# A four-stage transformer block on one core: the multiplication in the row quantisation moved from VectorE to GpSimd

## The chip, the cores and the metric

The kernel runs on one core of a Trainium2 chip (trn2). The metric is the device time of one execution in microseconds (us), the median over the runs. Engines: TensorE (PE in the profile, with its weight loads as PEld), VectorE (DVE), ScalarE (ACT), GpSimd (POOL) and SyncE (SP), which issues the DMAs here. Each has its own instruction stream, and they meet through semaphores.

## The reference

Eight batches of 512 rows x 512 columns pass through four layers, each with a layer norm ahead of it and a residual sum behind it:

```python
x = x + L0_xattn(layernorm(x), ctx, mask)      # 16 heads of 32, 77 keys
x = x + L0_ffn(layernorm(x), packed ternary w) # rows quantised to 8 bits
x = x + L1_xattn(layernorm(x), ctx)            # 16 heads of 64, 77 keys
x = x + L1_ffn(layernorm(x), w_freq)           # product with a matrix in frequency space
```

The second layer is the one that the change touches. For each row:

```python
act_scale = 127.0 / max(max(abs(x)), 1e-5)
x_dq = clip(round(x * act_scale), -128.0, 127.0) / act_scale
y = x_dq @ w.T + bias                          # w is ternary times one scale
```

## The kernel before

A batch has four tiles of 128 rows (t = 0 to 3). All other layers split their operands into a high and a low float16 part and multiply three times (`products`, lines 167 to 172); the ternary layer multiplies small whole numbers in bfloat16, once.

**Order of the work.** The program is a hand-written schedule. A batch's round has 18 slots (`NS`), and each engine walks through the same list `SLOTS` in its own program. Slots 0 to 7 have a unit of the first attention (stage X), slots 10 to 17 one of the second attention (stage Y, of the batch before), slots 8 and 9 none. A unit is a tile's scores for half of the heads: scores on TensorE, maxima on VectorE, exponentials on ScalarE, sums on VectorE, normalisation on GpSimd (`normalise`, line 644), a high part on ScalarE (line 783), a low part on VectorE (line 1180) or, for units in `LOW_BY_POOL`, on GpSimd (line 649), then a transposing DMA. `FILLS` puts matrix products into the slots, and their results are drained one slot later, by ScalarE and VectorE or by VectorE alone (the residual sum, line 1112, with the row statistics, line 1052 and `ln_group`, lines 1058 to 1068).

**Layer norms.** VectorE makes the variance, GpSimd the reciprocal root and the shift (`rstd_of`, lines 635 and 637). The tables `APPLY`, `LOWER` and `BIAS` say in which slot a pair of tiles is normalised, lowered and given its bias. An entry is (j, pair): j is the layer (0 to 3), the pair 0 means tiles 0 and 1, the pair 2 means tiles 2 and 3. For j = 1, the quantised layer, `APPLY` and `LOWER` have (1, 0) in slot 8 and (1, 2) in slot 13. `BIAS` has (1, 0) in slot 9 and (1, 2) together with (2, 2) in slot 13, four additions of 128x512 on GpSimd (line 666).

**The quantisation.** ScalarE writes the normalised rows of a pair into `xn` (line 800; 128 x 2 x 512 float32; one buffer for all layers). VectorE's `quantise` (lines 1070 to 1085) finds the largest magnitude of each row (line 1077), bounds it (1078), makes the scale for the result (1079), the reciprocal (1080) and the step (1081), multiplies each tile by its step and adds the rounding constant (1083, two instructions), and takes the constant off again, with the bound at 127, while it writes bfloat16 into `xh` (1085). `step` is a fence: the instruction raises a semaphore and VectorE waits for it. The last one raises `ln_lowered`, for which SyncE's transposing DMA into `qiT` waits (line 522), and behind that TensorE's product (line 1337).

**GpSimd's slot.** It does, in this order: normalise the unit of the slot before; `rstd_of`; the rows that it normalises itself (`rows`, line 657, a tensor-scalar of 128x512 with a column for each operand, into the same `xn`); the low part of the unit two slots back; the biases. In slot 8 the `rstd_of` is that of the next batch's first layer norm, for whose variance VectorE works just ahead of `quantise`.

Of the kernel before, what the change touches and what calls it, by code (L numbers as in the profile page):

```python
# [9 lines left out]
ALU = mybir.AluOpType  # L10
# [137 lines left out]
def listed(table, g):  # L148

    i, s = SLOTS[g]  # L150
    out = [(j, pair, i - ln_lag(j, pair)) for j, pair in table.get(s, [])]
    return [e for e in out if there(e[2])]
# [7 lines left out]
GROUPS = {(j, b, t): n for n, (j, t0, w, b) in enumerate(sum((groups_at(g) for g in range(len(SLOTS))), [])) for t in range(t0, t0 + w)}  # L160
APPLIED = {e: n for n, e in enumerate(sum((listed(APPLY, g) for g in range(len(SLOTS))), []))}
POOL_ROWS = {e: n for n, e in enumerate([e for e in APPLIED if e[:2] in ROWS_BY_POOL])}
FIRST_ROWS = [e for e in APPLIED if e[0] == 0 and e[2] == 0]
BIASED = {e: n for n, e in enumerate(sum((listed(BIAS, g) for g in range(len(SLOTS))), []))}

# [81 lines left out]
def layers(nc, k, x, scr_k0, scr_k1, scr_v0, scr_v1, out, inputs):  # L247

    here = ExitStack()
    with here:  # L250
# [3 lines left out]
        def sem(name):  # L254
            return here.enter_context(nc.semaphore(name))
# [39 lines left out]
        ln_var, rstd_ready, ln_ready, ln_applied, ln_lowered, biased = (sem(n) for n in (  # L295
            "ln_var", "rstd_ready", "ln_ready", "ln_applied", "ln_lowered", "biased"))
        rows_ready = sem("rows_ready")
        rows_turned = [sem(f"rows_turned{i}") for i in range(2)]
        absmax_ready, allmax_ready, scale_ready, hi_done, lo_done = (sem(n) for n in (
            "absmax_ready", "allmax_ready", "scale_ready", "hi_done", "lo_done"))  # L300
# [122 lines left out]
        def unit_at(g):  # L423

            return SLOT_UNIT[g] if 0 <= g < len(SLOTS) else None
# [181 lines left out]
        def _(pool):  # L607
# [44 lines left out]
            def rows(j, pair, b):  # L652
# [4 lines left out]
                    ins = pool.tensor_scalar(xn[:, t - pair, :], xs(b)[:, t, :], rstd[:, j, t:t + 1], shift[:, j, t:t + 1], ALU.mult, ALU.add)  # L657
                ins.then_inc(rows_ready, 1)

            def add_bias(j, pair, b):  # L660
                pool.wait_ge(ln_lowered if (j, pair) in ROWS_BY_DVE else ln_applied, APPLIED[j, pair, b] + 1)
                if (j, pair) in ROWS_BY_POOL:
                    pool.wait_ge(rows_ready, POOL_ROWS[j, pair, b] + 1)
                bias = {1: "bf0", 2: "bo", 3: "bf1"}[j]
                for t in (pair, pair + 1):
                    ins = pool.tensor_tensor(xs(b)[:, t, :], xs(b)[:, t, :], k[bias][:, :], ALU.add)  # L666
                ins.then_inc(biased, 1)
# [17 lines left out]
            for g, (i, s) in enumerate(SLOTS):  # L685
                if unit_at(g - 1):
                    normalise(*unit_at(g - 1))
                if (i, s) == (0, 0):
                    all_reduce("WQ1")
                if (i, s) == (1, 4):  # L690
                    all_reduce("WO")
                for e in groups_at(g):
                    if e[0] != 0 or e[3] != 0:
                        rstd_of(*e)
                for e in later(APPLY, g):
                    if e[:2] in ROWS_BY_POOL:
                        pool.wait_ge(ln_ready, GROUPS[e[0], e[2], e[1]] + 1)
                        rows(*e)
                if unit_at(g - 2) and unit_at(g - 2)[:2] in LOW_BY_POOL:
                    probs_low(*unit_at(g - 2))  # L700
                for e in listed(BIAS, g):
                    add_bias(*e)

# [153 lines left out]
        def _(dve):  # L857
# [212 lines left out]
            def quantise(t, b):  # L1070
# [7 lines left out]
                step(dve.tensor_scalar(amax[:, pair], amax[:, pair], 1e-5, None, ALU.max))  # L1078
                dve.tensor_scalar(cscale[:, pair], amax[:, pair], f[:, F_WSC:F_WSC + 1], None, ALU.mult)
                step(dve.reciprocal(ascale[:, pair], amax[:, pair]))  # L1080
                step(dve.tensor_scalar(ascale[:, pair], ascale[:, pair], 127.0, None, ALU.mult))
                for j in (t, t + 1):
                    ins = dve.tensor_scalar(xn[:, j - t, :], xn[:, j - t, :], ascale[:, j:j + 1], MAGIC, ALU.mult, ALU.add)  # L1083
                step(ins)
                dve.tensor_scalar(quantised(n), xn[:, :, :], MAGIC, 127.0, ALU.subtract, ALU.min).then_inc(ln_lowered, 1)

            def rows_low(j, pair, b):
# [433 lines left out]
```

## Time and profile before

| | |
|---|---|
| median of 3 runs | 1170.33 us (1170.12 to 1173.37) |
| the profiled execution's time | 1169.09 us |
| its span in the trace | 1167.3 us |
| mean granted TensorE clock | 0.91 |
| PE busy | 957.4 us (82%) |
| DVE busy | 898.2 us (77%) |
| ACT busy | 634.9 us (54%) |
| POOL busy | 492.7 us (42%) |

The rows are all of the one profiled execution; its time is 1.2 us under the median, and its span leaves out 1.8 us around it. A batch's round takes some 110 us in the middle of the run: the early calls of `quantise` for batches 4 and 5 start at 635.25 and 743.51 us. Busy shares are averages over stages with different limits, so the chain of waits and the rows in order of time tell more. In a row of the timeline the bracket at the end is the idle time of the engine before it and what ended that.

### The profile page before, as it was taken

Reading aid. Unit: us, or ns where it says so; the run is one execution under the profiler, and the core shown is the slowest. Engines: PE = TensorE matmul, PEld = TensorE weight load, DVE = VectorE, ACT = ScalarE, POOL = GpSimd, SP = SyncE. Lnnn points to the kernel's source line nnn. Section 1 sums busy time; section 2 is a strip of 40 time slices with the busy share of each in tenths; the row PEclk is TensorE's granted clock in tenths of the full one; section 3 lists DMA queues with packets and bytes.
Section 4 is the critical chain, followed back from the end, with each engine's and each line's share of the span. In section 5 each row is a group of like instructions: output and inputs, shape, how many; then the busy total and the mean of one; then the engine's idle time right before and its main releaser. Section 6 shows DMA issues by size and latency. Waiting matters only on the chain.

```text
span 1167.3 us, 17877 instructions
## 1 busy us (share of the span) xinstructions
PE 957.4 (82%) x6211; PEld 508.7 (44%) x6227; DVE 898.2 (77%) x1704; ACT 634.9 (54%) x1748; POOL 492.7 (42%) x437
## 2 busy tenths in 40 slices
PE   1896994693777997898799889979997898599694
PEld 0443463352343554454454445544554455344341
DVE  8777379537989799979987998899789978835732
ACT  2333174233577658657763776477558656614701
POOL 0224024111646267337723762475267336802603
PEclk9988997895699998999899989989998999699797
DMA  9623025543846747585648656746856483551612
GB/s 368 195 86 108 1 67 137 121 116 74 144 88 105 134 84 128 96 167 110 116 102 146 100 107 122 147 89 120 141 110 123 90 143 69 111 103 25 118 39 72
DMA packets 379026, 131.95 MB, mean 113 GB/s; under 512 B 365148, under 2 KB 370812, under 8 KB 375609
## 3 DMA queue, kind: packets, MB, share of 16 engines
q1 hardware_dynamic: 378937, 130.82, 54.7%
q8 instruction: 49, 0.80, 0.3%
q14 instruction: 40, 0.33, 0.1%
HBM read 35.14 MB, written 15.96 MB: 44 GB/s over the span
## 4 chain that ended last, share of the span: by engine, by line
DVE 35%; PE 24%; DMA 10%; ACT 9%; POOL 8%; SPq 8%; issue 7%; ACTq 0%; POOLq 0%; DVEq 0%
PE wb L170 6%; PE wb L171 6%; PE wb L172 6%; DMA prT<-ph 6%; DVE ph L1180 4%; ACT pr L770 3%; DVE mx L1158 3%; SPq L494 3%; PE wb L1307 2%; DVE xr L1112 2%; DVE stats L1052 2%; POOL xr L666 2%; DVE xn L1083 2%; DVE parts L862 2%; ACT xn L800 2%
## 5 line engine op out<-in xcount | busy, mean ns | idle before, releaser
L644 POOL TENSOR_TENSOR pr<-pr,sm 128x616 f32<-128x616 f32 x128 | 166.1, 1298 | 289.9 <-DVE sm L1175 283.0
L770 ACT ACTIVATE pr<-scores,mx,factor 128x77 f32<-128x77 f32 x576 | 229.6, 425 | 21.6 <-DVE mx L1161 18.4
L170 PE MATMUL wb<-xT,wq_hl 128*128 128x512 f16 x384 | 150.8, 393 | 9.6 <-DVE qc L1105 4.2
L171 PE MATMUL wb<-xT,wq_hl 128*128 128x512 f16 x384 | 150.6, 392 | 0.0
L172 PE MATMUL wb<-xT,wq_hl 128*128 128x512 f16 x384 | 149.6, 390 | 0.0
L783 ACT ACTIVATE ph<-pr 128x618 f16<-128x618 f32 x128 | 93.5, 732 | 97.0 <-DMA prT<-ph 75.6
L635 POOL TENSOR_TENSOR rstd<-var,mhalf 128x2 f32<-128x2 f32 (+1 forms) x48 | 51.2, 1067 | 221.4 <-DVE var L1068 221.4
L770 ACT ACTIVATION_READ_ACCUMULATOR pr<-scores,mx,factor 128x1 f32 x576 | 123.9, 215 | 0.0
L1112 DVE SCALAR_TENSOR_TENSOR xr<-wb,factor,xr 128x512 f32<-128x512 f32 x72 | 53.3, 740 | 71.7 <-PE wb L172 71.7
L1158 DVE TENSOR_REDUCE mx<-scores 128x8 f32<-128x616 f32 x128 | 101.1, 790 | 5.7 <-PE scores L172 5.6
L170 PE MATMUL scores<-k1b,qc 128*128 128x154 f16 x256 | 61.0, 256 | 49.3 <-DVE qc L1105 29.1
L170 PE MATMUL wb<-wo_hl,qc 128*128 128x512 f16 x256 | 97.1, 379 | 0.0
L172 PE MATMUL wb<-wo_hl,qc 128*128 128x512 f16 x256 | 97.1, 379 | 0.0
L171 PE MATMUL wb<-wo_hl,qc 128*128 128x512 f16 x256 | 97.1, 379 | 0.0
L730 ACT ACTIVATE qc<-wb,bq_s 128x512 f16<-128x512 f32 x64 | 43.7, 686 | 81.6 <-PE wb L172 81.6
L774 ACT ACTIVATE pr<-pr,factor 128x616 f32<-128x616 f32 x56 | 45.4, 811 | 76.5 <-DVE pr L1166 76.4
L1096 DVE TENSOR_TENSOR xh<-xn,xh 128x1024 f16<-128x1024 f32 x48 | 69.4, 1446 | 20.4 <-ACT xh L797 9.9
L1180 DVE SCALAR_TENSOR_TENSOR ph<-pr,ph 128x618 f16<-128x618 f32 x80 | 83.4, 1043 | 1.0 <-ACT ph L783 0.7
L1307 PE MATMUL wb<-prT,v1b 103*64 103x512 f16 x576 | 72.1, 404 | 10.3 <-DMA prT<-ph 8.0
L797 ACT ACTIVATE xh<-xr,shift,rstd 128x512 f16<-128x512 f32 x72 | 56.1, 804 | 39.0 <-POOL shift L637 26.7
L666 POOL TENSOR_TENSOR xr<-xr,bf_b 128x512 f32<-128x512 f32 x48 | 72.9, 1539 | 8.2 <-ACT xh L797 7.1
L1337 PE MATMUL wb<-tern,qiT 128*128 128x512 bf16 x112 | 38.8, 475 | 38.5 <-DMA qiT<-xh 21.2
(218 smaller groups left out, 2502.6 us busy)
## 6 DMA issues: line engine op xcount, KB each, us to landing
xr<-in_x SPq DMA_DIRECT2D x6, 1024.0 KB, 6.1
out_x<-xr SPq DMA_DIRECT2D x6, 1024.0 KB, 5.2
prT<-in_dft SPq DMA_DIRECT2D x1, 3072.0 KB, 22.2
k1b<-scr_k SPq DMA_DIRECT2D x16, 154.0 KB, 6.8
scr_v<-k1b SPq DMA_DIRECT2D x9, 256.0 KB, 3.2
scr_k<-k1b SPq DMA_DIRECT2D x7, 308.0 KB, 3.1
xr<-in_wf SPq DMA_DIRECT2D x2, 1024.0 KB, 10.6
x<-in_x SPq DMA_DIRECT2D x2, 1024.0 KB, 10.7
```

The lines of the kernel that those rows point to most:

```text
L170: pe.matmul(out, lhs(0), rhs(0), start=start, stop=False, **kw)
L171: pe.matmul(out, lhs(0), rhs(1), start=False, stop=False, **kw)
L172: return pe.matmul(out, lhs(1), rhs(0), start=False, stop=stop, **kw)
L644: pool.tensor_tensor(v, v, s, ALU.mult).then_inc(probs_ready, 1)
L666: ins = pool.tensor_tensor(xs(b)[:, t, :], xs(b)[:, t, :], k[bias][:, :], ALU.add)
L770: ins = act.activation(pr[U % 3][:, h // 4, cols], sc[:, U % 2, h // 4, cols], ACT.Exp, bias=mx[:, U % 4, h:h + 1], scale=k["factor"][:, f ...
L783: act.activation(ph[:, U % 2, 0, :, :, 0:CH], pr[U % 3][:, :, 0:GKP].rearrange("p g (c n) -> p g c n", c=3), ACT.Copy, scale=1.0 if (stage ...
L1096: dve.tensor_tensor(xh[:, n % 2, :, 1, :], xn[:, :, :], xh[:, n % 2, :, 0, :], ALU.subtract).then_inc(ln_lowered, 1)
L1112: dve.scalar_tensor_tensor(out=xs(b)[:, t, :], in0=wb[:, n % WB, :], scalar=factor, in1=xs(b)[:, t, :], op0=ALU.mult, op1=ALU.add).then_in ...
L1158: step(dve.tensor_reduce(m, s, AX.X, ALU.max))
L1180: dve.scalar_tensor_tensor(out=ph[:, U % 2, 1, :, :, 0:CH], in0=pr[U % 3][:, :, 0:GKP].rearrange("p g (c n) -> p g c n", c=3), scalar=PS, ...
L1307: return pe.matmul(bank[column:column + H1, :], v1b[0:CH, h, g, slot, :], prT[0:CH, :, g // 2, h1, g % 2, c, :], start=start, stop=stop, s ...
```

## The change

GpSimd gets a function `round_rows` that does the two multiplications of a pair in place in `xn`. VectorE raises `step_known` with the step and then waits for `rows_rounded`. In GpSimd's slot the new call stands behind the low part and ahead of the biases. The table `QUANTISED` only counts the calls.

```diff
+QUANTISED = {e[1:]: n for n, e in enumerate([e for e in sum((listed(LOWER, g) for g in range(len(SLOTS))), []) if e[0] == 1])}
...
+        step_known, rows_rounded = sem("step_known"), sem("rows_rounded")
...
+            def round_rows(t, b):
+                pool.wait_ge(step_known, QUANTISED[t, b] + 1)
+                for j in (t, t + 1):
+                    ins = pool.tensor_scalar(xn[:, j - t, :], xn[:, j - t, :], ascale[:, j:j + 1], MAGIC, ALU.mult, ALU.add)
+                ins.then_inc(rows_rounded, 1)
...
                 if unit_at(g - 2) and unit_at(g - 2)[:2] in LOW_BY_POOL:
                     probs_low(*unit_at(g - 2))
+                for j, pair, b in later(LOWER, g):
+                    if j == 1:
+                        round_rows(pair, b)
                 for e in listed(BIAS, g):
                     add_bias(*e)
...
                 step(dve.reciprocal(ascale[:, pair], amax[:, pair]))
-                step(dve.tensor_scalar(ascale[:, pair], ascale[:, pair], 127.0, None, ALU.mult))
-                for j in (t, t + 1):
-                    ins = dve.tensor_scalar(xn[:, j - t, :], xn[:, j - t, :], ascale[:, j:j + 1], MAGIC, ALU.mult, ALU.add)
-                step(ins)
+                dve.tensor_scalar(ascale[:, pair], ascale[:, pair], 127.0, None, ALU.mult).then_inc(step_known, 1)
+                dve.wait_ge(rows_rounded, QUANTISED[t, b] + 1)
                 dve.tensor_scalar(quantised(n), xn[:, :, :], MAGIC, 127.0, ALU.subtract, ALU.min).then_inc(ln_lowered, 1)
```

GpSimd's order in slot 13 (the pair (1, 2) of a batch in the middle of the run) was, from the low part of a unit on through the biases of layers 1 and 2 to the next slot's normalisation:

```order
L649 TENSOR_TENSOR ph<-pr,ph 128x6x103 [waits probs_hi]
L666 TENSOR_TENSOR xr<-xr,bf_b 128x512 [waits ln_applied]
L666 TENSOR_TENSOR xr<-xr,bf_b 128x512
L666 TENSOR_TENSOR xr<-xr,bo_b 128x512 [waits ln_applied]
L666 TENSOR_TENSOR xr<-xr,bo_b 128x512
L644 TENSOR_TENSOR pr<-pr,sm 128x2x308 [waits sums_ready]
```

and is now, with every line number of GpSimd's program 2 to 8 higher:

```order
L651 TENSOR_TENSOR ph<-pr,ph 128x6x103 [waits probs_hi]
L665 TENSOR_SCALAR xn<-xn,ascale 128x512 [waits step_known]
L665 TENSOR_SCALAR xn<-xn,ascale 128x512
L674 TENSOR_TENSOR xr<-xr,bf_b 128x512 [waits ln_applied]
L674 TENSOR_TENSOR xr<-xr,bf_b 128x512
L674 TENSOR_TENSOR xr<-xr,bo_b 128x512 [waits ln_applied]
L674 TENSOR_TENSOR xr<-xr,bo_b 128x512
L646 TENSOR_TENSOR pr<-pr,sm 128x2x308 [waits sums_ready]
```

The four additions and all behind them now stand behind the wait for the step. VectorE's end of `quantise` in slot 13 and the next unit's first operations were:

```order
L1079 TENSOR_SCALAR cscale<-amax,factor 128x2 [waits dve_step]
L1080 RECIPROCAL ascale<-amax 128x2
L1081 TENSOR_SCALAR ascale<-ascale 128x2 [waits dve_step]
L1083 TENSOR_SCALAR xn<-xn,ascale 128x512 [waits dve_step]
L1083 TENSOR_SCALAR xn<-xn,ascale 128x512
L1085 TENSOR_SCALAR xh<-xn 128x1024 [waits dve_step]
L1158 TENSOR_REDUCE mx<-scores 128x8 [waits scores_full]
```

and are now:

```order
L1090 TENSOR_SCALAR cscale<-amax,factor 128x2 [waits dve_step]
L1091 RECIPROCAL ascale<-amax 128x2
L1092 TENSOR_SCALAR ascale<-ascale 128x2 [waits dve_step]
L1094 TENSOR_SCALAR xh<-xn 128x1024 [waits rows_rounded]
L1167 TENSOR_REDUCE mx<-scores 128x8 [waits scores_full]
```

Two instructions left VectorE, and its last one of the call waits for GpSimd.

## Rows read from the trace of the kernel before

**Rows 1.** The page's part 4: the chain that ended last, shares by engine
```profile
DVE 35%; PE 24%; DMA 10%; ACT 9%; POOL 8%; SPq 8%; issue 7%; ACTq 0%; POOLq 0%; DVEq 0%
```
**Rows 2.** The chain in order of time, whole run (start us, us, what)
```profile
633.72 1.51 ACT xn L800 x2
```
**Rows 3.** The same chain, 606 to 680 us (batch 4, both calls)
```profile
637.25 0.90 DVE xn L1083 x2
...
641.14 0.07 issue
...
668.45 1.85 DVE xn L1083 x2
...
671.05 3.08 DMA qiT<-xh
```
**Rows 4.** Timeline, VectorE and GpSimd, early call, batch 4 (start us, us, engine...)
```profile
635.25 1.22 DVE L1077 TENSOR_REDUCE amax<-xn 128x2 f32<-128x1024 f32 x1 [2.37 <-ACT xn L800]
...
638.16 0.69 DVE L1085 TENSOR_SCALAR xh<-xn 128x1024 bf16<-128x1024 f32 x1
...
641.21 1.01 POOL L635 TENSOR_TENSOR rstd<-var,mhalf 128x4 f32<-128x4 f32 x1 [5.69 <-DVE var L1068]
```
**Rows 5.** Timeline, VectorE and GpSimd, late call and after, batch 4
```profile
664.36 1.20 DVE L1077 TENSOR_REDUCE amax<-xn 128x2 f32<-128x1024 f32 x1
...
667.29 1.12 DVE L1081 TENSOR_SCALAR ascale<-ascale 128x2 f32<-128x2 f32 x1
...
670.33 0.69 DVE L1085 TENSOR_SCALAR xh<-xn 128x1024 bf16<-128x1024 f32 x1
...
672.48 0.16 DVE L1174 TENSOR_SCALAR sm<-sm 128x8 f32<-128x8 f32 x1
...
674.61 0.17 DVE L1065 TENSOR_SCALAR mean<-mean 128x2 f32<-128x2 f32 x1
...
664.67 2.49 POOL L666 TENSOR_TENSOR x<-x,bf_b 128x512 f32<-128x512 f32 x2
667.12 2.49 POOL L666 TENSOR_TENSOR xr<-xr,bo_b 128x512 f32<-128x512 f32 x2
672.96 1.22 POOL L644 TENSOR_TENSOR pr<-pr,sm 128x616 f32<-128x616 f32 x1 [3.35 <-DVE sm L1175]
```
**Rows 6.** Instructions on tile xn (ns min/median/max, first and last start)
```profile
L657 POOL TENSOR_SCALAR xn<-xr,rstd,shift x36: 758/767/1417, 201.1 to 1142.2; 128x512 f32<-128x512 f32 x36
```
**Rows 7.** Timeline, early call of batch 1, and a VectorE row released by GpSimd
```profile
314.58 1.69 DVE L1085 TENSOR_SCALAR xh<-xn 128x1024 bf16<-128x1024 f32 x1
...
314.16 1.56 POOL L649 TENSOR_TENSOR ph<-pr,ph 128x618 f16<-128x618 f32 x1 [0.82 <-ACT ph L783]
...
1006.82 0.80 DVE L1166 TENSOR_TENSOR pr<-scores,mx 128x616 f32<-128x616 f32 x1 [0.57 <-POOL ph L649]
...
1004.42 2.30 POOL L649 TENSOR_TENSOR ph<-pr,ph 128x618 f16<-128x618 f32 x1
```
**Rows 8.** Timeline, both calls of batch 0
```profile
194.70 2.59 POOL L649 TENSOR_TENSOR ph<-pr,ph 128x618 f16<-128x618 f32 x2
...
200.22 0.69 DVE L1085 TENSOR_SCALAR xh<-xn 128x1024 bf16<-128x1024 f32 x1
...
221.26 2.48 POOL L666 TENSOR_TENSOR x<-x,bf_b 128x512 f32<-128x512 f32 x2 [6.35 <-ACT xn L800]
...
222.73 1.05 DVE L1078 TENSOR_SCALAR amax<-amax 128x2 f32<-128x2 f32 x1
...
225.26 0.69 DVE L1085 TENSOR_SCALAR xh<-xn 128x1024 bf16<-128x1024 f32 x1
```
**Rows 9.** TensorE's waits; windows (busy of PE, PEld, DVE, ACT, POOL; clock; DMA; GB/s)
```profile
639.58 0.39 PE L170 MATMUL wb<-xT,wq_hl 128*128 128x512 f16 x1 [1.25 <-DVE xr L1112]
...
674.26 1.86 PE L1337 MATMUL wb<-tern,qiT 128*128 128x512 bf16 x4 [3.18 <-DMA qiT<-xh]
...
639.50:642.00 2.50, 2.42 (x12) 1.13 (x13) 2.36 (x11) 0.00 (x0) 0.79 (x1) 1.00 0.64 120
674.20:680.00 5.80, 5.74 (x22) 3.00 (x23) 5.59 (x16) 5.79 (x17) 4.73 (x6) 0.50 0.31 65
```

## The prediction

> **What bounds the kernel now.** I read the chain of waits first, because no engine is busy all the time. It passes from engine to engine and spends its largest share on VectorE [rows 1]. So a microsecond of VectorE counts where the chain is on VectorE, and one of GpSimd only where VectorE or the chain waits for it. I then read the chain in order of time over one batch, to see where the quantisation lies on it. Each batch calls `quantise` twice: for rows 0 and 1 in slot 8 (the **early call**) and for rows 2 and 3 in slot 13 (the **late call**). The chain enters the early call from ScalarE's normalised rows in batches 2 to 6, five times (one of them in [rows 2]), runs through its multiplication [rows 3] and on by the residual sum and the row statistics to GpSimd. It also runs through the late call [rows 3]; in batches 4 and 5 it leaves by the transposing DMA to TensorE, in batches 1, 2, 3, 6 and 7 it stays on VectorE. Last I set the VectorE and GpSimd rows of both calls side by side (batch 4 stands for all). In the early call GpSimd is idle and VectorE's operations go at their own length [rows 4]. In the late call GpSimd adds biases for 5 us and VectorE's tensor-scalars are stretched: from the start of the reduction to the start of the last operation it is 5.97 us, against 2.91 us in the early call [rows 4, 5]. The 3.06 us between them are waiting inside VectorE's rows. The reader should see how: a tensor-scalar of VectorE that starts while a GpSimd operation runs ends only about when that one does (the 1.12 us row on two numbers per partition), and it never happens while GpSimd is idle.
>
> **The change, part by part.**
> *Removed from VectorE*: per call two 128x512 multiplications and the fence behind them, 0.90 us [rows 3] when alone.
> *Added to GpSimd*: per call two operations of the same shape. The nearest row is GpSimd's own tensor-scalar of 128x512 float32, 0.767 us each [rows 6]; with one constant instead of a second column I take the same, so 1.53 us.
> *Added waits*: VectorE to GpSimd costs 0.07 us [rows 3]; back, 0.10 us: the VectorE row that waited for GpSimd starts at 1006.82, the GpSimd operation ended at 1004.42 + 2.30 = 1006.72 [rows 7]. Behind VectorE's wait stands its whole program; behind GpSimd's, in the late call, stand four bias additions.
>
> *Early call, batches 2 to 6.* GpSimd is idle there, its next work waits for VectorE anyway. VectorE's path from the end of the step to the last operation was 0.90 us and becomes 0.07 + 1.53 + 0.10 = 1.70 us; less some 0.05 us for the fences that go with it, **+0.75 us** each, on the chain: +3.75 us. Bounds: +0.2 us if GpSimd did it at VectorE's own 0.45 us a piece [rows 3], +1.7 us if it took as long as its two-input additions, 1.25 us (half of a pair in [rows 5]). I take the row of its own form, which lies between them.
>
> *Early call, batch 1.* GpSimd's next operation there, the low part of another unit, ran at 314.16 and the last operation of the call beside it, 1.69 us instead of 0.69 [rows 7]. The step is known at about 313.65 (0.93 us, two multiplications and a fence, ahead of that operation); the rounding then lasts to 315.25; the low part (1.30 us, half of [rows 8]'s pair) starts at once, VectorE 0.10 us later and so behind it: end about 317.2 against 314.58 + 1.69 = 316.27, +0.9 us.
>
> *Early call, batch 0.* Two low parts and two bias additions of GpSimd lie on it, and the call ends at 200.22 + 0.69 = 200.9 [rows 8]. Now GpSimd waits after the first low part, which ends at 196.0 (half of the pair); the step follows two small operations later, 196.3, rounding to 197.9, second low part to 199.2, last operation to 199.9: -1.05 us. Batch 0, late call: there are only two additions, from 221.26, and they stretch one small operation to 1.05 us; the call ends at 225.26 + 0.69 = 225.95 [rows 8]. Now the step is known 0.9 us earlier, at 223.45, the rounding ends at 225.05, and the last operation waits for the first addition behind it, 225.05 + 1.25 + 0.69 = 227.0: +1.0 us. These two cancel. In batch 7 the chain is on TensorE at the early call: 0.
>
> *Late call, the others.* GpSimd now stands still until the step is known, so the reduction and the small operations run at their own length: the step is ready 1.96 us after the start, at 666.3 instead of 668.4. The rounding ends at 667.9. Then the four bias additions that had run from 664.67 [rows 5] start, without a pause, as GpSimd's operations do back to back in those rows; VectorE needs 0.10 us to notice, and its last operation waits for the first addition: end at 667.9 + 1.25 + 0.69 = 669.8, against 670.33 + 0.69 = 671.02. **The stretch of 3.06 us becomes a gain of 1.2 us at this point**, for the rounding costs 1.7 instead of 1.85 with its stretch, and the last operation takes the wait over. What is late next: the other additions now run from 669.1, held up 0.7 us by VectorE's last operation (the 1.56 us row of [rows 7] shows such a hold-up), to about 673.5, instead of being over at 669.6. VectorE's next small tensor-scalar, at 672.48 before [rows 5], comes at 671.3 into the third addition and ends at 672.4, 0.25 us ahead; the one in the row statistics, at 674.61 before, comes at 674.35 under the normalisation of probabilities, which started at 672.96 and now starts at 673.5 and ends at 674.7. The lead is then 0 to 0.1 us. So on VectorE the gain is given back within one slot: -0.1 us in each of batches 1, 2, 3, 6 and 7, -0.5 us. By the transposing DMA the 1.2 us arrive at TensorE, which waited 3.18 us for it in batch 4 [rows 9]; but VectorE, 0.1 us ahead, is close behind TensorE there, so I take half, -0.5 us in each of batches 4 and 5, -1.0 us. Bounds for these seven: 0 and -8 us (the whole 1.2 us each).
>
> GpSimd's normalisation ends 0.5 us later and ScalarE with it; I found no wait behind it that this would lengthen. DMAs are neither added nor moved in any queue. Order on the other three engines is untouched.
>
> *Sum*: the terms in their order are +3.75 + 0.9 - 1.05 + 1.0 - 0.5 - 1.0 = **+3.1 us**. The profiled execution took 1169.09 us, so 1172.2 there; it lies 1.24 us under the median of the runs, which gives 1173.4 us against 1170.33.
>
> The Trainium skill, "GPSIMD Engine Reference", section 4.1 Engine selection, sends elementwise work to VectorE, but calls one-input operations on GpSimd "roughly line-rate". At 512 elements per partition that would be some 0.53 us for one operation (an estimate from that page's words and VectorE's 0.96 GHz), and the sum would be nearer +1 us, inside the forecast's own range. The row of this kernel says 0.767 us, and the sum goes by the row.
>
> **Rivals.**
> *A, VectorE gets in first (faster).* Decides: whether the last operation of the late call starts before GpSimd's first bias addition. Then it ends at 668.7 and not 669.8, and with the same working the lead after the row statistics is about 1.1 us: seven late calls -7.7 us; batch 0 early -2.2 and late 0, batch 1 early -0.3, the five early calls +3.75: -6.4 us, 1163.9. Against it: the additions need no semaphore that is open by then, and follow back to back in [rows 5], while VectorE has to be woken over 0.10 us. The Trainium skill, "SBUF — State Buffer", section Who interferes with whom, says that the two engines share a port pair as an exclusive lock, and that whoever issues first holds it for its whole instruction; the 1.69 us of [rows 7] agree with it. Chance 0.14.
> *B, TensorE loses its clock at the early call (slower, well beyond the forecast).* TensorE waits 1.25 us for VectorE's residual sum there [rows 9], which becomes 2.0 us; it kept the full clock (1.00, 2.4 GHz) behind 1.25 us but ran at the level of 1.2 GHz (0.50) for 5.8 us behind 3.18 us [rows 9]. 5.8 us at half clock are 2.9 us lost; five times on the chain, with the +3.1, gives up to 1188. From which wait on the clock falls no row between 1.25 and 3.18 us says; 2.0 is nearer the harmless one. Chance 0.12.
> *C, the waits are hidden.* The chain was beside other paths with as much length, and the 0.75 us vanish in slack, as would the lead of the late calls: 1170.3. For it: in batch 7 it is TensorE's. Against it: five of eight batches have it on the chain. Chance 0.12.
> *D, TensorE gains at the late call.* Its wait of 3.18 us shrinks to 2.0 us and in batches 4 and 5 the 5.8 us at half clock [rows 9] go away: -2.9 us twice, 1167.6. Chance 0.12.
>
> **How the numbers follow.** Forecast 0.50, between 1170 and 1177 by its bounds. A measurement of this kernel can tell about 0.3%, 3.5 us: faster is below 1166.8, slower above 1173.8. The forecast lies just inside "same": 0.28 same, 0.22 slower. A gives 0.12 faster and 0.02 same, B 0.12 slower, C 0.10 same and 0.02 faster, D 0.06 each of faster and same. Together faster 0.20, same 0.46, slower 0.34. The range goes from the better part of A to the lower half of B: 1164.5 to 1180.
>
> **What would show it.** After the change: the early call's last operation starts about 3.7 us after the reduction's start (2.91 now); the late call's ends about 5.5 us after it (6.66 now) and shows 1.7 to 1.9 us instead of 0.69 as its own length; the small tensor-scalar that follows shows about 1.1 us instead of 0.16; GpSimd's rounding rows show 0.77 us. A last operation of 0.69 us in the late call means rival A. A granted clock of 0.5 right behind the early call means B, and none behind the late one D. If the GpSimd row is far from 0.77 us, the sum is off from its first term.

## The result, and the profile after

| | before | change |
|---|---|---|
| median, measured side by side | 1172.53 us (16 runs, 1169.38 to 1177.05) | 1176.31 us (16 runs, 1173.82 to 1179.00) |
| ratio to before | | 1.0034, 95% interval 1.0021 to 1.0046 |
| the profiled execution | 1169.09 us, span 1167.3, clock 0.910 | 1176.54 us, span 1174.2, clock 0.907 |

The change makes the kernel slower by 0.34%, 3.8 us, just over what a measurement of it can tell from nothing. The forecast was a sum of +3.1 us, called just inside "same". The size is close; the reason turned out to be another one. The two profiled executions lie 6.9 us apart, more than the medians: a profile shows where time goes, and the medians say how much. Of the executions timed below, one of the kernel e3_bias14 took 2022.66 us and is left out of its row.

The page of the kernel after, its parts 1 and 4 (engines; shares of the chain by engine, against [rows 1]):

```profile
PE 960.9 (82%) x6211; PEld 508.8 (43%) x6227; DVE 880.6 (75%) x1672; ACT 636.1 (54%) x1748; POOL 522.1 (44%) x469
...
DVE 33%; PE 25%; POOL 11%; ACT 8%; DMA 8%; issue 7%; SPq 7%; POOLq 0%; ACTq 0%; DVEq 0%
```

VectorE lost 17.6 us of busy time, GpSimd gained 29.4 us, and the chain moved the same way: VectorE 35% to 33%, GpSimd 8% to 11%. So VectorE has less to do and the kernel is slower; the share of an engine answers nothing here.

The new instructions of GpSimd, from the view of one source line of the kernel after:

```profile
L665 POOL TENSOR_SCALAR xn<-xn,ascale x32: 690/691/696, 196.6 to 1000.0; 128x512 f32<-128x512 f32 x32
its engine sat idle before it (us, times) until:
  DVE ascale L1092: 28.5, 16
who waited for it (us, times):
  DVE xh L1094: 24.0, 16
```

One takes 0.691 us, to within 6 ns in all 32, not the 0.767 us of GpSimd's normalisation [rows 6]. VectorE waited 24.0 us for it in 16 calls, 1.5 us each.

The early call of batch 4, timeline of VectorE and GpSimd of the kernel after (against [rows 4]):

```profile
639.12 1.22 DVE L1088 TENSOR_REDUCE amax<-xn 128x2 f32<-128x1024 f32 x1 [2.45 <-ACT xn L811]
...
640.91 0.17 DVE L1092 TENSOR_SCALAR ascale<-ascale 128x2 f32<-128x2 f32 x1
642.58 0.69 DVE L1094 TENSOR_SCALAR xh<-xn 128x1024 bf16<-128x1024 f32 x1 [1.50 <-POOL xn L665]
...
641.18 1.36 POOL L665 TENSOR_SCALAR xn<-xn,ascale 128x512 f32<-128x512 f32 x2 [1.87 <-DVE ascale L1092]
```

From the reduction to the last operation it is 3.46 us, against 2.91 us: +0.55 us. The step ends at 641.08, GpSimd starts 0.10 us later, and VectorE starts 0.04 us after GpSimd's 642.54.

Batch 4 does not stand for all early calls. In batch 3 GpSimd is at a low part when the kernel after calls `quantise`, and stretches a small operation from 0.17 to 1.00 us:

```profile
528.66 1.00 DVE L1089 TENSOR_SCALAR amax<-amax 128x2 f32<-128x2 f32 x1
...
528.33 1.32 POOL L651 TENSOR_TENSOR ph<-pr,ph 128x618 f16<-128x618 f32 x1
```

Before, that happened in the early calls of batches 2 and 5, after, in those of batches 2, 3 and 5. From the end of the step on it is +0.55 us in all of them, but batch 3's call as a whole got 1.35 us longer.

The late call of batch 4 and what follows, the same view (against [rows 5]):

```profile
668.82 1.20 DVE L1088 TENSOR_REDUCE amax<-xn 128x2 f32<-128x1024 f32 x1
...
670.59 0.17 DVE L1092 TENSOR_SCALAR ascale<-ascale 128x2 f32<-128x2 f32 x1
672.25 1.75 DVE L1094 TENSOR_SCALAR xh<-xn 128x1024 bf16<-128x1024 f32 x1 [1.50 <-POOL xn L665]
...
675.46 0.92 DVE L1183 TENSOR_SCALAR sm<-sm 128x8 f32<-128x8 f32 x1
...
678.01 0.77 DVE L1073 TENSOR_TENSOR mean<-stats 128x2 f32<-128x2 f32 x1
...
678.95 0.17 DVE L1076 TENSOR_SCALAR mean<-mean 128x2 f32<-128x2 f32 x1
...
670.86 1.36 POOL L665 TENSOR_SCALAR xn<-xn,ascale 128x512 f32<-128x512 f32 x2 [1.69 <-DVE ascale L1092]
672.18 2.94 POOL L674 TENSOR_TENSOR x<-x,bf_b 128x512 f32<-128x512 f32 x2
675.08 2.50 POOL L674 TENSOR_TENSOR xr<-xr,bo_b 128x512 f32<-128x512 f32 x2
677.54 1.22 POOL L646 TENSOR_TENSOR pr<-pr,sm 128x616 f32<-128x616 f32 x1
```

The reader should see four things. The step, which had stretched to 1.12 us, is at its own 0.17 us. The last operation has the stretch now, 1.75 us instead of 0.69, since GpSimd's first addition starts at 672.18 and VectorE's operation at 672.25. The call ends at 674.00, 5.18 us after its start, against 6.66 us. And the lead of 1.48 us is gone behind it: two small operations took 0.92 us beside the third addition and 0.77 us beside the normalisation behind them, and the first tensor-scalar of the row statistics stands 10.13 us after the call's start, against 674.61 - 664.36 = 10.25 us before. In both calls of this batch the local picture is the predicted one.

What had not been looked at is TensorE behind the late call. Some 30 us behind the late call's start TensorE has done the 36 products of the second attention's probabilities with its values (slot 17) and waits until VectorE has drained one of their output banks; then it starts the ternary product of the fourth tile. Its row of batch 4, and a window of 4 us from 30.0 us behind the call's start. Columns of a window: length, busy PE, PEld, DVE, ACT, POOL, granted clock, DMA share, GB/s. The kernel before:

```profile
694.32 0.81 PE L1337 MATMUL wb<-tern,qiT 128*128 128x512 bf16 x3 [1.76 <-DVE qc L1103]
...
694.36:698.36 4.00, 4.00 (x22) 2.11 (x22) 3.86 (x13) 3.99 (x18) 0.61 (x2) 1.00 0.72 137
```

The kernel after, and the stretch that answers to [rows 9]'s half clock:

```profile
698.46 1.06 PE L1346 MATMUL wb<-tern,qiT 128*128 128x512 bf16 x2 [3.72 <-DVE qc L1112]
...
678.82:684.82 6.00, 5.87 (x35) 2.79 (x32) 5.83 (x14) 6.00 (x18) 5.21 (x6) 1.00 0.32 62
...
698.82:702.82 4.00, 4.00 (x14) 1.93 (x13) 3.60 (x12) 2.46 (x11) 0.33 (x1) 0.50 0.36 68
```

After [rows 9]'s wait of 3.18 us for the transposing DMA TensorE ran at the 1.2 GHz level. In the kernel after, that wait is no longer there and the clock is 1.00 in that stretch. But TensorE, earlier now (its 36 products end 25.9 us behind the call's start, not 28.2), waits 3.72 us instead of 1.76 us at the next place, for a bank that VectorE frees only 0.3 us earlier, and behind it the clock is at 0.50: 14 matmuls in 4 us where there had been 22. Round 4 (from batch 4's late call to batch 5's) takes 111.6 us after and 109.1 us before.

The half clock about the late call did not go away in batch 4, though, it moved forward. These windows go from 4 us ahead of the call's start to 16 us behind it, before and after:

```profile
660.36:680.36 20.00, 13.04 (x64) 7.10 (x65) 18.52 (x36) 15.24 (x50) 13.70 (x13) 0.74 0.70 120
...
664.82:684.82 20.00, 16.12 (x80) 8.56 (x80) 17.07 (x34) 15.25 (x49) 15.61 (x15) 0.74 0.70 121
```

The mean clock is 0.74 in both, and TensorE does 80 matmuls in place of 64. Nor is batch 4 the typical one. Mean granted clock in that window, in the one from 26 to 40 us behind the call's start, and the round:

| batch | about the call: before, after | 26 to 40 us: before, after | round: before, after |
|---|---|---|---|
| 2 | 0.74, 0.74 | 1.00, 0.76 | 108.3, 110.7 us |
| 3 | 0.74, 0.83 | 0.76, 0.88 | 111.8, 110.9 us |
| 4 | 0.74, 0.74 | 1.00, 0.76 | 109.1, 111.6 us |
| 5 | 0.74, 0.91 | 1.00, 0.88 | 110.1, 111.1 us |
| 6 | 0.74, 0.74 | 0.88, 1.00 | 106.4, 105.7 us |

Both kernels have as much half clock in these windows, some 62 us in the five batches. What differs is the place: about the late call or behind the wait at 30 us. Before, the second place has it in batches 3 and 6, after, in batches 2 to 5. The wait of 1.76 us was one of batches 4 and 5 only; in batches 2, 3 and 6 it was 3.53 to 3.71 us already before the change.

The starts of the last late call are 989.92 us before and 997.26 us after; from there to the end of the span it is 177.4 and 176.9 us. So the difference of the two profiles arises in the rounds: +1.3, +2.2, +2.4, -0.9, +2.6, +0.9 and -0.6 us for those of batches 0 to 6.

### The profile page after: what moved, and what is told of

Its sections match the earlier page's. It is cut to its first block, busy times and chain, and to the rows that moved or that the text cites. A ratio compares the mean times of both kernels' runs of the same rounds, so it can differ in the third digit from the quotient of the medians.

```text
span 1174.2 us, 17877 instructions
## 1 busy us (share of the span) xinstructions
PE 960.9 (82%) x6211; PEld 508.8 (43%) x6227; DVE 880.6 (75%) x1672; ACT 636.1 (54%) x1748; POOL 522.1 (44%) x469
## 4 chain that ended last, share of the span: by engine, by line
DVE 33%; PE 25%; POOL 11%; ACT 8%; DMA 8%; issue 7%; SPq 7%; POOLq 0%; ACTq 0%; DVEq 0%
PE wb L171 7%; PE wb L172 6%; PE wb L173 6%; DVE ph L1189 3%; ACT pr L781 3%; DVE mx L1167 3%; DVE stats L1063 3%; SPq L496 3%; PE wb L1316 3%; DMA prT<-ph 3%; POOL xr L674 2%; DVE xh L1105 2%; DVE parts L873 2%; DVE xr L1121 2%; POOL xn L665 2%
## 5 line engine op out<-in xcount | busy, mean ns | idle before, releaser
L1105 DVE TENSOR_TENSOR xh<-xn,xh 128x1024 f16<-128x1024 f32 x48 | 72.7, 1515 | 21.5 <-ACT xh L808 9.9
L674 POOL TENSOR_TENSOR xr<-xr,bf_b 128x512 f32<-128x512 f32 x48 | 75.5, 1594 | 8.0 <-ACT xh L808 7.1
L1063 DVE BATCH_NORM_STATS2 stats<-xr 128x6 f32<-128x512 f32 x96 | 64.7, 690 | 4.4 <-DMA xr<-in_x 1.8
```

The lines of the kernel that those rows point to most:

```text
L1063: last = dve.bn_stats(stats[:, j, t, :], xs(b)[:, t, :])
L1105: dve.tensor_tensor(xh[:, n % 2, :, 1, :], xn[:, :, :], xh[:, n % 2, :, 0, :], ALU.subtract).then_inc(ln_lowered, 1)
```

## The experiments

Theories, all made after the result, and the third only after the first four runs. **Theory 1**: the handover in the early calls is the loss. **Theory 2**: the loss is in the late call, where GpSimd stands still until the step is known, so that its additions and what follows come later. Beside it stands the prediction's rival A: the stretched last operation keeps the gain away. **Theory 3**: each local gain or loss only moves TensorE against VectorE, and what it costs is the clock behind TensorE's wait 30 us behind the late call. Rounds, waits and dips are read from one profiled execution of each kernel. "Dip" below is a stretch of a granted clock of about 0.5 there. Every kernel was timed beside the kernel before, whose medians there were 1172.83 us (e1 to e9) and 1173.48 us (e10 to e12). They ran in three groups on different chips, so across groups the ratios are what to compare.

| run | what | median (runs) | ratio to before, 95% interval |
|---|---|---|---|
| the change | | 1176.31 (16) | 1.0034, 1.0021 to 1.0046 |
| e1_early | only the early call moved | 1177.81 (6) | 1.0044, 1.0027 to 1.0060 |
| e2_late | only the late call moved | 1176.41 (12) | 1.0033, 1.0018 to 1.0049 |
| e3_bias14 | before, biases one slot later | 1170.55 (11) | 0.9984, 0.9972 to 0.9997 |
| e4_dve_first | change, VectorE let in first | 1171.67 (12) | 0.9982, 0.9968 to 0.9995 |
| e6_after_bias14 | change, biases one slot later | 1178.60 (8) | 1.0045, 1.0030 to 1.0060 |
| e7_after_busy | change, some products twice | 1170.51 (12) | 0.9983, 0.9968 to 0.9998 |
| e8_before_busy | before, the same products twice | 1172.56 (12) | 0.9991, 0.9978 to 1.0003 |
| e9_bias6_14 | before, biases in slots 6 and 14 | 1169.26 (8) | 0.9969, 0.9953 to 0.9984 |
| e10_bias6_14_busy | e9 with the products twice | 1165.31 (6) | 0.9940, 0.9918 to 0.9962 |
| e11_dve_first_busy | e4 with the products twice | 1166.49 (10) | 0.9953, 0.9938 to 0.9968 |
| e12_early_busy | e1 with the products twice | 1171.68 (12) | 0.9995, 0.9981 to 1.0008 |

### The two halves of the change: e1_early and e2_late

`quantise` takes the new way only where t is 0 (e1) or 2 (e2), and GpSimd rounds only then:

```diff
+                if t == 0:
+                    dve.tensor_scalar(ascale[:, pair], ascale[:, pair], 127.0, None, ALU.mult).then_inc(step_known, 1)
+                    dve.wait_ge(rows_rounded, b + 1)
+                else:
+                    step(dve.tensor_scalar(ascale[:, pair], ascale[:, pair], 127.0, None, ALU.mult))
+                    for j in (t, t + 1):
+                        ins = dve.tensor_scalar(xn[:, j - t, :], xn[:, j - t, :], ascale[:, j:j + 1], MAGIC, ALU.mult, ALU.add)
+                    step(ins)
```

Expected of e1_early:

> Only the early call's multiplication (rows 0 and 1, slot 8) goes to GpSimd, the late call is as before. Theory 1 (the loss is the early call's handover of 0.55 to 0.75 us on the chain, the late call gives its gain back): the last operation of the early call starts 0.55 us later after the reduction, the late call is unchanged at 6.66 us, and the time is 3 to 4 us above before (ratio about 1.003), as large as the whole change's. Theory 2 (the loss is GpSimd's standing still in the late call, which delays its additions and the normalisation behind them): within 1 us of before.

Expected of e2_late:

> Only the late call's multiplication (rows 2 and 3, slot 13) goes to GpSimd. Theory 1: the call ends 1.47 us earlier after its start (5.19 instead of 6.66 us), the row statistics behind it only 0.1 us earlier, and the time is within 1.5 us of before (ratio 0.999 to 1.001). Theory 2: 3 to 4 us above before (1.003).

Measured: 1177.81 and 1176.41 us. The first is what theory 1 expected, and 1 us more, the second what theory 2 did, so neither can be the whole. Each half alone costs as much as both together. They do not add, which a sum of handovers and stretches would have to. Inside the calls each half does what it did in the change: e1's early call takes 0.55 us more and its late call 6.66 us as before, e2's late call 5.19 us. So the place of the loss is not in the calls. Both halves have what the change has, a wait 30 us behind the late call (2.74 to 3.71 us) with, mostly, a dip behind it; batch 4 of e2_late, timeline and window:

```profile
698.91 1.06 PE L1352 MATMUL wb<-tern,qiT 128*128 128x512 bf16 x2 [3.71 <-DVE qc L1118]
...
699.28:703.28 4.00, 4.00 (x14) 1.97 (x13) 3.59 (x12) 2.45 (x11) 0.34 (x1) 0.50 0.38 72
```

In e1_early there is a dip in all of batches 2 to 6, in e2_late in batches 2, 4, 5 and 6. Their longest rounds, 113.8 and 112.8 us, are round 5 of each, and there the clock falls a second time: behind the early call of batch 6, after waits of TensorE of 2.61 and 2.11 us. That is the prediction's rival B, which the change itself shows nowhere in batches 2 to 6.

The rounds can be sorted by it. In the kernels before and after, e1, e2 and e4 (below), rounds 2 to 5 with a dip take 111.1 us on average (16 rounds), those without one 109.1 us (4 rounds). A dip goes with some 2 us.

### Taking GpSimd out of the late call: e3_bias14, and on the change: e6_after_bias14

The same line in both:

```diff
-BIAS = {9: [(1, 0)], 10: [(3, 0)], 13: [(1, 2), (2, 2)], 15: [(3, 2)], 16: [(2, 0)]}
+BIAS = {9: [(1, 0)], 10: [(3, 0)], 14: [(1, 2), (2, 2)], 15: [(3, 2)], 16: [(2, 0)]}
```

Expected of e3_bias14:

> The kernel before, with the biases of slot 13 (four additions on GpSimd) moved to slot 14; no multiplication moves. If the 3.06 us by which the late call is longer than the early one are VectorE waiting for GpSimd's additions, the late call takes 3.6 to 3.9 us instead of 6.66 in every batch, with all its rows at their own length. What the time does depends on where the additions land: GpSimd's next normalisation is up to 5 us later. If that is hidden, 5 to 15 us below before; if it is on the chain, 5 us or more above.

Expected of e6_after_bias14:

> The whole change with the additions of slot 13 moved to slot 14, so that nothing of GpSimd stands behind the rounding of the late call. The last operation shows 0.69 us and the late call takes 4.15 us, as the early one. Against the kernel before with the additions in slot 14 it has both handovers of 0.55 us and nothing in return: 4 to 9 us above that kernel (some 1175 to 1180).

e3_bias14, late call of batch 4 (timeline, VectorE):

```profile
664.03 1.20 DVE L1077 TENSOR_REDUCE amax<-xn 128x2 f32<-128x1024 f32 x1
665.26 0.17 DVE L1078 TENSOR_SCALAR amax<-amax 128x2 f32<-128x2 f32 x1
665.47 0.23 DVE L1079 TENSOR_SCALAR cscale<-amax,factor 128x2 f32<-128x2 f32 x1
665.60 0.16 DVE L1080 RECIPROCAL ascale<-amax 128x2 f32<-128x2 f32 x1
665.80 0.17 DVE L1081 TENSOR_SCALAR ascale<-ascale 128x2 f32<-128x2 f32 x1
666.92 0.69 DVE L1085 TENSOR_SCALAR xh<-xn 128x1024 bf16<-128x1024 f32 x1
```

The call takes 3.58 us instead of 6.66, every row at its own length: the 3.06 us in VectorE's rows of [rows 5] were waiting for GpSimd's additions. The row statistics end 7.67 us after the call's start instead of 10.74. That is some 3 us earlier per batch in seven batches, and 0.9 us in batch 0, and the kernel gains 2 us in all (0.9984), which is neither of the outcomes expected. On the change the same edit loses instead of gains: 1.0045, with the late call at 4.12 us. In that profile the last late call starts 4.0 us earlier than in the change (993.28 against 997.26), and the stretch behind it is 4.4 us longer (181.3 us against 176.9). In e3_bias14 it is long too, 180.5 us. Why the end of the run grows when batch 7's biases come a slot later I did not find; it stays open.

e9_bias6_14 moves the two pairs to different slots, 6 and 14:

```diff
-BIAS = {9: [(1, 0)], 10: [(3, 0)], 13: [(1, 2), (2, 2)], 15: [(3, 2)], 16: [(2, 0)]}
+BIAS = {6: [(2, 2)], 9: [(1, 0)], 10: [(3, 0)], 14: [(1, 2)], 15: [(3, 2)], 16: [(2, 0)]}
```

> The kernel before with the additions of slot 13 taken apart: the attention's bias (2,2) goes to slot 6 of the same round, where GpSimd waits, the quantised layer's bias (1,2) to slot 14. The late call takes 3.6 us in place of 6.66 as with both moved to slot 14, and GpSimd's next normalisation is 2.5 instead of 5 us later. 3 to 8 us below before.

Measured 0.9969, the end 174.8 us long and the late call at 3.58 us. But its rounds 2 to 5 take 109.3, 110.8, 109.2 and 110.1 us, not less than before's 108.3, 111.8, 109.1 and 110.1: there is a wait of 3.3 us and a dip in all of them.

### Letting VectorE in first: e4_dve_first (rival A)

GpSimd waits, behind its rounding, for that rounding to be written, before it goes on to the additions:

```diff
                 ins.then_inc(rows_rounded, 1)
+                pool.wait_ge(rows_rounded, QUANTISED[t, b] + 1)
```

> The whole change, and GpSimd waits for its own rounding semaphore before it goes on, so that VectorE's last operation starts before GpSimd's first addition (rival A of the prediction made true). If it does, the last operation of the late call shows 0.69 us instead of 1.75, the late call ends at about 4.2 us instead of 5.19 after its start, and the row statistics 1 us earlier than with the change. By the prediction's rival A that is worth about 7 to 9 us against the change as made (some 4 us below before); if the lead is lost again behind the call, within 2 us of the change.

Late call of batch 4, timeline of VectorE and GpSimd:

```profile
663.40 1.20 DVE L1089 TENSOR_REDUCE amax<-xn 128x2 f32<-128x1024 f32 x1
...
666.84 0.69 DVE L1095 TENSOR_SCALAR xh<-xn 128x1024 bf16<-128x1024 f32 x1 [1.49 <-POOL xn L665]
...
673.88 0.16 DVE L1080 TENSOR_TENSOR var<-var,half 128x2 f32<-128x2 f32 x1
...
666.89 2.99 POOL L675 TENSOR_TENSOR x<-x,bf_b 128x512 f32<-128x512 f32 x2
```

Now VectorE starts 0.05 us ahead of the addition and takes 0.69 us, and GpSimd's pair shows the hold-up, 2.99 us instead of 2.49 [rows 5]. The call ends 4.13 us after its start. Yet the variance is ready 10.64 us after it, where the change has 10.63: the additions behind take this lead too. So rival A's mechanism works and its price of 1.1 us per late call doesn't arrive. The kernel is nevertheless 4.6 us faster than the change by the medians, some 6 us by the ratios. In the profiles 3.6 us of it lie between the late calls of batches 0 and 1 (117.4 us against 121.0), where the early call, too, ends 1.1 us earlier (5.24 against 6.35 us). So the stretched last operations cost something, but in batches 0 and 1 and not round by round. How 1.1 us there become 3.6 us no run shows.

### Holding the clock: e7_after_busy and e8_before_busy

The last 18 of the 36 products of probabilities with values that TensorE does just ahead of the long wait are done twice (`pair` in this edit counts output banks, not tiles), in the change (e7) and in the kernel before (e8). The first results are overwritten by the second; TensorE has about 2 us more to do per batch.

```diff
+                if pair == 2:
+                    for n, (h, h1) in enumerate(((0, 0), (0, 1), (1, 0))):
+                        head(o, 0, 0, h, h1, 0, n == 0, n == 2)
+                        head(o, H1, 1, h, h1, 0, n == 0, n == 2)
...
```

Expected of e7_after_busy:

> The whole change, and TensorE does the 18 products of the third and fourth output bank of the second attention twice (the second time from scratch, so the result is the same). It makes TensorE busy for 2 us more in the stretch in which it waits 3.5 to 3.7 us per round for VectorE's drain, some 26 to 29.5 us behind the start of the late call. Theory 3 (the change loses by TensorE's clock there: the late call's transpose now arrives early, TensorE no longer waits at +10 us, runs ahead, and waits once and longer at +29.5 us, behind which its clock is at 0.5 for 4 to 6 us on the chain): the wait is 1.5 to 2 us, the granted clock behind it is 1.00 in all rounds, and the time is 5 to 9 us below the change's in spite of the added work. Theory 1 (only the handover counts): no gain, 0 to 5 us above the change.

Expected of e8_before_busy:

> The kernel before with the same added products. Theory 3: in the profile of before the clock falls behind this wait in two or three rounds of five, so the gain is half as large, 2 to 5 us below before. Theory 1: 0 to 5 us above before.

e7_after_busy, batch 4, the same row and window as above:

```profile
693.24 1.04 PE L1356 MATMUL wb<-tern,qiT 128*128 128x512 bf16 x4 [1.37 <-DVE qc L1112]
...
694.00:698.00 4.00, 4.00 (x24) 2.15 (x22) 3.86 (x13) 2.89 (x13) 0.69 (x1) 1.00 0.36 68
```

The wait is 1.37 us, the clock 1.00, 24 matmuls in 4 us instead of 14. The wait is 1.36 or 1.37 us without a dip in all of batches 2 to 6, in both kernels. With more work for TensorE the change is 5.8 us faster, at 0.9983. Its rounds 2 to 5 take 109.2, 109.3, 109.0 and 109.5 us, where the change had 110.7, 110.9, 111.6 and 111.1: 7.2 us less together, of which 3.6 us are given back behind the last late call (180.5 us against 176.9), perhaps because batch 7's doubled products find no such wait to lie in.

The kernel before with the same products is at 0.9991, no more than 1 us below before, where theory 3 had expected 2 to 5 us. Its rounds 2 to 5 are 108.7, 108.9, 108.8 and 109.2 us, 3.7 us less together than before's, most of it in round 3, the one with a dip; behind the last late call it is 4.5 us longer (181.8 us against 177.3), so that little is left. With the clock held at this place in both, the change is not slower than the kernel before: 0.9983 against 0.9991, and the intervals overlap. Its rounds are 0.3 to 0.5 us longer, near the early call's 0.55 us. TensorE's busy time points the same way: the same 144 added matmuls raise it by 12.5 us in the kernel before (957.4 to 969.9) and by 5.0 us in the change (960.9 to 965.9).

This pair speaks for theory 3: with the wait filled, the 3.8 us are gone. Two limits remain. The products shorten the wait and remove the dip at once, so no run holds the clock and leaves the wait as it is. And the mean granted clock of a whole execution doesn't show the loss: it is 0.912 in the 16 executions of the change and 0.912 in the 77 of the kernel before beside e1 to e12, and it rises to 0.921 in e7 and 0.918 in e8. As in the table by batch, the clock of batches 2 to 6 is at 0.50 for as long before as after, and it is the place that would have to make the difference; e8 is at 0.50 for as long as before about every late call, and its rounds are short.

### With the clock held: e12_early_busy, e11_dve_first_busy, e10_bias6_14_busy

The edits are those of e1, e4 and e9, each with the products twice.

Expected of e12_early_busy:

> Only the early call's rounding by GpSimd, and the 18 output products of pair 2 done twice. If the clock made the early call's part of the change dear (1177.8 us without the added products), then here the clock is 1.00 in all rounds and what is left is the handover, 0.5 us in each of five or six batches, +3 us on the 1172.6 of the kernel before with the same products less what batches 0 and 1 gain: 1172 to 1176 us. If the handover itself costs more than its own length, over 1177 us with the clock at 1.00.

Measured 0.9995 where the early half without the products was at 1.0044. Rounds 2 to 5: 109.1, 109.5, 109.2, 109.3 us. It stands with e8_before_busy's 0.9991; the early call's handovers, 0.55 us each, are not to be told from nothing in the whole, though its rounds are 0.1 to 0.6 us longer than e8's. Theory 1 falls as the main cause.

Expected of e11_dve_first_busy:

> The change with VectorE let in ahead of the bias additions (GpSimd waits for its own rounding to be written first), and the 18 output products of pair 2 done twice. Theory, that the lead of the late call is lost behind it to the other bias additions and that the clock costs the rest: like the change with the products twice, 1170.5 us, or 1 us under it through batches 0 and 1; clock 1.00, rounds 109 us. Rival A of the prediction, that getting in first is worth 1.1 us per batch once nothing else hides it: 1163 to 1166 us, rounds 108 us.

Measured 0.9953, against e7's 0.9983: rival A's time, near enough, but not by its mechanism. Rounds 2 to 5 are 109.2, 109.5, 109.1 and 109.4 us, e7's to 0.2 us. The gain lies before them, between the late calls of batches 0 and 1: 117.8 us against 120.9. My theory's expectation, 1 us under e7, was too small.

Expected of e10_bias6_14_busy (its "wait for the operands of pair 2" is the wait for an output bank of above):

> The kernel before with the biases of rows 2 moved to slots 6 and 14, and the 18 output products of pair 2 done twice. If the clock behind TensorE's wait for the operands of pair 2 is what keeps the short late call (3.6 us) from paying, then the clock stays at 1.00 in all rounds here and the late call's 3 us show at least in part: rounds 107 to 108 us against 109.8 in the run with the moved biases alone and 108.8 in the kernel before with the products twice, so 1162 to 1167 us. If the batches are bound by the chain on VectorE wherever the clock stands, rounds stay near 108.8 and the time is 1169 to 1172 us.

e10, window of batch 4 behind the same wait:

```profile
693.44:697.44 4.00, 4.00 (x25) 2.25 (x23) 3.86 (x12) 2.40 (x11) 1.20 (x1) 1.00 0.23 44
```

Measured 0.9940, the best of all: it beats the kernel before by 7 to 8 us and the change by 11 us. Its rounds 2 to 5 are 108.2, 108.3, 108.2 and 108.9 us, 1.5 us below e9's on average, and 0.5 us below e8's. So a call that is 3 us shorter is worth about 0.5 us per round even with the clock held; the time came in as the theory had it, the rounds were between the two expectations. It still does 18 products twice per batch; work of use in their place would be better, and wasn't tried.

## Why the prediction was right or wrong

- **The early call, +0.75 us in batches 2 to 6.** Measured +0.55 us. The term that was mis-sized is GpSimd's instruction: 0.691 us and not 0.767, so 1.36 us (the pair overlaps a little) and not 1.53. That row "of its own form" has a column for each operand, the new instruction a column and a constant. The Trainium skill, "GPSIMD Engine Reference", section 4.1 Engine selection, calls one-input operations "roughly line-rate"; the trace has 0.691 us for 512 elements where VectorE needed 0.45 us [rows 3], so it agrees only roughly. And "batch 4 stands for all" was a misreading: GpSimd was not idle in the early calls of batches 2 and 5, where it stretched a small operation, and with the change it stretches one in batch 3 as well, +1.35 us for that call in all.
- **The handovers, 0.07 and 0.10 us.** Measured 0.10 and 0.04 us in the early call, 0.10 and 0.03 us in the late one. Together 0.14 instead of 0.17 us.
- **Batches 0 and 1.** Batch 0 early: end 6.35 us after the start against 7.65, -1.3 us (forecast -1.05). Batch 0 late: +0.7 us (+1.0). Batch 1 early: +0.66 us (+0.9). Right in sign and order.
- **The late call.** Gain at its end 1.47 us (1.2), last operation 1.75 us long (1.7 to 1.9), lead at the row statistics 0.12 us (0 to 0.1). The whole course of it held, rival A's condition did not (VectorE was 0.07 us too late). The Trainium skill, "SBUF — State Buffer", section Who interferes with whom, has the port pair go to whoever issues first, for a whole instruction; the trace and e4_dve_first agree with it in both directions, 1.75 us behind by 0.07 us and 0.69 us ahead by 0.05 us.
- **Batches 4 and 5, -0.5 us each through the transposing DMA.** This is the step that failed. It took "VectorE is close behind" for a loss of half the lead, and looked no further. Batch 5 shows the course most plainly, for there the first wait was only shortened (two rows of the kernel before, then two of the kernel after):

```profile
783.32 1.87 PE L1337 MATMUL wb<-tern,qiT 128*128 128x512 bf16 x4 [3.16 <-DMA qiT<-xh]
803.46 0.81 PE L1337 MATMUL wb<-tern,qiT 128*128 128x512 bf16 x3 [1.76 <-DVE qc L1103]
...
788.99 1.02 PE L1346 MATMUL wb<-tern,qiT 128*128 128x512 bf16 x4 [1.79 <-DVE xr L1121]
810.05 1.49 PE L1346 MATMUL wb<-tern,qiT 128*128 128x512 bf16 x3 [3.63 <-DVE qc L1112]
```

The 1.4 us that TensorE gains at the first wait it loses again at the second, 20 us later, which grows from 1.76 to 3.63 us (3.72 in batch 4), and the clock falls behind it. Rounds 4 and 5 became 2.6 and 0.9 us longer, not 0.5 us shorter. For round 2, +2.4 us with a wait of 3.53 us before and 3.71 us after, the prediction had no term at all; there too a dip is new.
- **Rival D.** Its sign came: no half clock right behind the late call's DMA in batches 4 and 5. Its gain did not. In batch 4 the half clock stands further forward instead, and in both batches a dip behind the wait at 30 us is new.
- **Rival B, the clock.** The right resource at the wrong place. At the early call TensorE's wait went from 1.25 to 1.69 us in batch 4, and in the 6 us behind it the granted clock was 1.00 as before. The prediction asked only about the wait that the change lengthens directly.
- **The sum.** +3.1 us forecast, +3.8 measured, and the near hit is partly luck. With the products doubled, the change and the early half stand at -0.08% and +0.04% of e8, each to some 0.2%, where the local terms of +3.1 us would be +0.26%; rounds 2 to 5 of both are 1.5 us longer than e8's in all. The rest of the 3.8 us came with the wait and the dips behind it, which the sum had at nothing.
- **Kept apart from it.** 1173.4 us and 1176.3 us differ by more than the two sums, because the kernel before itself ran at 1172.53 us in the comparison and not at 1170.33.

Open: why the end of the run grows by 3 to 4 us in e3_bias14 and e6_after_bias14; whether the wait alone, without the dip, would cost anything; and what besides the length of the wait decides on a dip. In batches 2 to 6 of the kernel before a wait of 3.53 us had no dip behind it and one of 3.71 us had; in the kernel after one of 3.53 us had a dip and one of 3.54 us had none; in e1_early waits of 2.74 and 2.83 us had one. The waits of 1.36 and 1.37 us, 25 in the five kernels with doubled products, never had one, nor had the two of 1.76 us.

## What to carry to other kernels

When an edit shifts two engines against each other, follow the one that gains until it meets its next wait, and read the granted clock behind that wait, before and after: a lead that ends in a longer idle of TensorE can cost more than it brought. Do it for every round, for one batch may not stand for all, and stretch by stretch, for the mean clock of a whole run can stay the same. If two halves of a change cost as much each as both together, look for an effect that is there or not there, and not for a term of a sum. To test for it, fill the wait with work that is already there: if the kernel gets faster with more work, it was the wait or the clock behind it that cost the time.

## What the runs showed of the hardware

- Doing 18 matmuls of a batch twice made the change faster by 0.51%, the early half by 0.49% and e9_bias6_14 by 0.29% (there the intervals overlap), and the kernel before by nothing that can be told.
- Who comes first by 0.05 us decides on 1.06 us: VectorE's tensor-scalar of 1024 elements takes 1.75 us when GpSimd's addition started 0.07 us ahead of it, 0.69 us when it started 0.05 us behind.
- GpSimd's tensor-scalar of 512 float32 elements took 0.691 us (690 to 696 ns in 32 instructions) with one column and a constant, and 0.767 us with two columns [rows 6].
- A second half-clock stretch stands in nearly every round of both kernels about the start of the late call, behind a wait of 4.3 us for VectorE (4.31 us in batch 4 before, 4.36 us after). It was there with and without the change, and with the doubled products: mean clock 0.74 from 4 us ahead of the call's start to 16 us behind it in batches 2 to 6 before, 0.74 to 0.91 after. Whether it costs time can't be seen: in rounds 2 to 5 e8_before_busy has 0.74 there and rounds of 108.7 to 109.2 us, e7_after_busy 0.83 and 109.0 to 109.5 us.
